# Last stage: GpSimd's whole copy of the odd stack replaced by transfers from two queues

## What is computed

```python
x = x + _L0_conv_ref(_gn(x), ...)     # masked convolution along rows, then a recurrence over the 32 rows
x = x + _L1_conv_ref(_gn(x), L1_conv_W, L1_conv_b, 4)

is3x3 = (i - n) % p == 0              # p = 4: output channel n and input channel i of one class
Wm = W * where(is3x3, full 3x3, centre tap only)
y = conv(x, Wm, padding 1) + sum(b, axis=1)
```

## Time and profile before

| | us |
|---|---|
| three runs | 640.96, 640.69, 638.35 |
| median | 640.69 |
| the profiled execution | 638.67 |
| its span, first to last instruction | 636.9 |
| around the span | 1.8 |
| GpSimd busy in the span | 405.2 |
| TensorE busy in the span | 581.3 |

### The profile page before, as it was taken

One profiled execution on the slowest core, in us unless ns is written; L12 is line 12 of the kernel. 1 busy time (PEld: TensorE's weight loads), 2 busy tenths in 40 slices (PEclk: granted clock), 3 DMA queues, 4 the chain that ended last, 5 costly groups with the idle time before them and its releaser, 6 DMA issues.

```text
span 636.9 us, 19612 instructions
## 1 busy us (share of the span) xinstructions
PE 581.3 (91%) x7741; PEld 381.7 (60%) x7741; DVE 504.3 (79%) x1183; ACT 488.9 (77%) x871; POOL 405.2 (64%) x373
## 2 busy tenths in 40 slices
PE   1799979799999999999999999996799999999995
PEld 0344435378888888878888888884443444343432
DVE  4689884379999999999999999998886686766440
ACT  2579859799999999999999999997374654636440
POOL 1379848545555555554555555554479999999991
PEclk9799979999999999999999999997899999999998
DMA  9988940004124444134442244400057465664755
GB/s 222 263 231 265 238 67 1 4 3 67 35 34 67 67 67 63 31 42 67 67 68 39 30 67 66 68 2 1 21 121 178 114 161 148 142 167 116 172 127 151
DMA packets 89659, 61.47 MB, mean 97 GB/s; under 512 B 73952, under 2 KB 75232, under 8 KB 89568
## 3 DMA queue, kind: packets, MB, share of 16 engines
q1 hardware_dynamic: 88608, 58.90, 44.2%
q10 hardware_dynamic: 960, 1.31, 0.8%
HBM read 35.07 MB, written 16.78 MB: 81 GB/s over the span
## 4 chain that ended last, share of the span: by engine, by line
PE 58%; POOL 23%; DVE 8%; ACT 5%; issue 3%; SPq 1%; DMA 1%; POOLq 0%; DVEq 0%; ACTq 0%
PE ps L1190 18%; PE ps L1168 13%; POOL stack L878 11%; PE ps L1195 9%; PE ps L1172 6%; POOL stack L874 6%; POOL stack L873 5%; PE ps L1113 4%; PE ps L1114 4%; DVE bn L465 2%; SPq L307 1%; PE ps L1290 1%; DMA img<-in_x_dram 1%; PE ps L1248 1%; POOL lo L817 1%
## 5 line engine op out<-in xcount | busy, mean ns | idle before, releaser
L836 POOL TENSOR_TENSOR fc<-gate,cell 128x352 f32<-128x352 f32 (+16 forms) x96 | 83.8, 873 | 142.7 <-ACT gate L978 142.7
L1190 PE MATMUL ps<-z_hi,wg_hi 128*128 128x352 f32 (+13 forms) x384 | 134.0, 350 | 3.1 <-ACT z_hi L962 3.1
L1190 PE MATMUL ps<-z_hi,wg_lo 128*128 128x352 f32 (+13 forms) x384 | 122.1, 319 | 0.0
L1195 PE MATMUL ps<-z_lo,wg_hi 128*128 128x352 f32 (+13 forms) x384 | 107.4, 320 | 0.0
L978 ACT ACTIVATE gate<-ps,gate_bias 128x352 f32<-128x352 f32 (+16 forms) x192 | 104.1, 542 | 1.1 <-PE ps L1195 0.9
L978 ACT ACTIVATE ps<-ps,gate_bias 128x352 f32<-128x352 f32 (+16 forms) x192 | 99.5, 518 | 0.0
L846 POOL TENSOR_TENSOR img<-hT,xr 128x352 f32<-128x352 f32 (+1 forms) x96 | 88.6, 923 | 5.7 <-DVE hT L682 5.6
L1034 ACT ACTIVATE img<-ps,finish 128x512 f32<-128x512 f32 x32 | 23.1, 773 | 88.5 <-PE ps L1290 80.4
L817 POOL TENSOR_TENSOR lo<-xn,hi 128x1024 f16<-128x1024 f32 x32 | 68.0, 2133 | 32.3 <-ACT hi L914 31.7
L465 DVE BATCH_NORM_STATS2 bn<-img 128x6 f32<-128x512 f32 x120 | 75.8, 681 | 5.1 <-DMA img<-in_x_dram 5.0
L1190 PEld LDWEIGHTS ps<-z_hi,wg_hi 128*128 128x128 f32 x384 | 72.3, 188 | 10.1 <-issue 2.6
(11 more groups left out here) (141 smaller groups left out, 1309.7 us busy)
## 6 DMA issues: line engine op xcount, KB each, us to landing
xr<-in_x_dram SPq DMA_DIRECT2D x64, 256.0 KB, 5.4
img<-in_x_dram SPq DMA_DIRECT2D x126, 128.0 KB, 3.4
out_dram<-img SPq DMA_DIRECT2D x62, 256.0 KB, 4.2
stack<-pad SPq DMA_DIRECT2D x46, 134.2 KB, 2.9
stack<-pad_first SPq DMA_DIRECT2D x14, 134.2 KB, 2.8
raw_c<-in_L_conv_W_dram SPq DMA_DIRECT2D x4, 144.0 KB, 3.0
out_dram<-img ACTq DMA_DIRECT2D x2, 256.0 KB, 4.6
img<-in_x_dram ACTq DMA_DIRECT2D x2, 128.0 KB, 3.5
```

What stands on the lines that cost most here:

```text
L836: pool.tensor_tensor(fc[it % 2][:, 0:c1 - c0], gate[it % 2][0][:, 0:c1 - c0], cell[:, c0:c1], ALU.mult).then_inc(fc_done, 1)
L1190: pe.matmul(gbank(it, m)[:, 0:n], w[:, GATE_ORDER[m], :], z_hi[it % 2][:, 0:n], start=(w is wg_hi), stop=False)
L1195: pe.matmul(gbank(it, m)[:, 0:n], wg_hi[:, GATE_ORDER[m], :], z_lo[it % 2][:, 0:n], start=False, stop=True).then_inc(gate_ready, 1)
```

## The change

Three things, all in the last stage, images 2 to 31:

- GpSimd no longer copies `pad` into the odd stack; per image it makes one whole copy and two quarter copies, all into the even stack.
- SyncE's two lowered quarters wait for `lo_done` of the image, and from image 6 on for `conv_done` of the buffer's last user, instead of for GpSimd's copy.
- ScalarE issues two new transfers per image (`stack_odds`): natural quarters 1 and 3 from `pad` into the odd stack, 32 partitions of 2,214 float16 each, with the same waits. They stand behind `norm` of the second image of each pair; for images 2 and 3 ahead of the first group's finish. TensorE waits for them with one more semaphore per buffer, `odd_in`.

The number of transfers for the stacks goes from 60 to 120; GpSimd's instructions go down by 30.

```diff
--- before.py
+++ after.py
@@ -260,7 +260,7 @@
         conv_done = sem("conv_done")
         class_set = sem("class_set")
         blocks_in = sem("blocks_in")
-        odd_stacked = sem("odd_stacked")
+        odd_in = [sem(f"odd_in{i}") for i in range(SLOTS)]
         even_stacked = sem("even_stacked")
         even_below = sem("even_below")
         below_in = [sem(f"below_in{i}") for i in range(SLOTS)]
@@ -409,7 +409,9 @@
 
             def stack_below(b):
 
-                sp.wait_ge(odd_stacked, b - PAIR + 1)
+                sp.wait_ge(lo_done, b + 1)
+                if b >= PAIR + SLOTS:
+                    sp.wait_ge(conv_done, (b - SLOTS) // PAIR + 1)
                 for q in ODD:
                     sp.dma_start(below(b, q), rows_below(b, q)).then_inc(below_in[b % SLOTS], 16)
 
@@ -869,10 +871,7 @@
                     pool.wait_ge(conv_done, (b - SLOTS) // PAIR + 1)
                 if b > PAIR:
                     pool.wait_ge(even_below, len(EVEN) * (b - PAIR))
-                evens, odds = stack[b % SLOTS]
-                pool.tensor_copy(odds[:].bitcast(F32), pad[b % SLOTS][:].bitcast(F32)).then_inc(odd_stacked, 1)
-                pool.tensor_copy(evens[:].bitcast(F32), pad[b % SLOTS][:].bitcast(F32)).then_inc(even_stacked, 1)
-                pool.wait_ge(odd_stacked, b - PAIR + 1)
+                pool.tensor_copy(stack[b % SLOTS][0][:].bitcast(F32), pad[b % SLOTS][:].bitcast(F32)).then_inc(even_stacked, 1)
                 pool.wait_ge(even_stacked, b - PAIR + 1)
                 for q in EVEN:
                     pool.tensor_copy(below(b, q).bitcast(F32), rows_below(b, q).bitcast(F32)).then_inc(even_below, 1)
@@ -1028,6 +1027,16 @@
                     act.wait_ge(lo_done, b - PAIR + 1)
                 whiten(rows(xn[b % PAIR][:]), b, chunk_of(b)[0] % 2, chunk_of(b)[1]).then_inc(xn_done, 1)
 
+            def stack_odds(b):
+
+                act.wait_ge(lo_done, b + 1)
+                if b >= PAIR + SLOTS:
+
+                    act.wait_ge(conv_done, (b - SLOTS) // PAIR + 1)
+                for q in ODD:
+                    r = slice(32 * q, 32 * q + 32)
+                    act.dma_start(stack[b % SLOTS][1][r], pad[b % SLOTS][r]).then_inc(odd_in[b % SLOTS], 16)
+
             def finish_class(g, q):
 
                 act.wait_ge(conv_done, g + 1)
@@ -1048,6 +1057,8 @@
             norm(2)
             high(3)
             norm(3)
+            stack_odds(2)
+            stack_odds(3)
             act.wait_ge(finish_done, 1)
             for g in range(GROUPS):
                 k = (g + 3) // 2
@@ -1067,6 +1078,8 @@
                 if near < B:
                     high(near + 1)
                     norm(near + 1)
+                    stack_odds(near)
+                    stack_odds(near + 1)
             act.wait_ge(out_act, len(ACT_CLASSES) * GROUPS)
             act.wait_ge(out_dve, len(DVE_CLASSES) * GROUPS)
             store_group(act, GROUPS - 1, range(2, Q))
@@ -1277,6 +1290,7 @@
 
                 for b in range(PAIR * g, PAIR * g + PAIR):
                     pe.wait_ge(below_in[b % SLOTS], 16 * len(ODD) * ((b - PAIR) // SLOTS + 1))
+                    pe.wait_ge(odd_in[b % SLOTS], 16 * len(ODD) * ((b - PAIR) // SLOTS + 1))
                 pe.wait_ge(even_below, len(EVEN) * (PAIR * g))
                 for m, (w, part) in enumerate(TERMS):
                     for e in range(3):
```

## The result

The changed kernel took 645.46 us (median of four runs, 641.14 to 649.22), beside 639.61 for the kernel before: a ratio of 1.010, 95% interval 1.0065 to 1.0135, so slower by 1%. Its profiled execution was the fastest of the four, 641.14 us with a span of 639.0, and shows less of the loss than the others had. The same kernel was therefore run and profiled once more among the experiments, with 643 to 647 expected of it: 644.76 us, ratio 1.0103 (1.007 to 1.0137), its profiled execution 644.98 with a span of 642.9. The first profile is called A1 here, the second A2. Before, the span was 636.9.

A forecast was written before the change was run, and what follows sets the result against it. GpSimd's copies were taken as the bound, TensorE only just behind: 6.3 us of waits go, less 0.7 (ScalarE) and 2.8 (program packets), 3.0 us with rounding up, from 640.69 to 637.7 us; range 633.5 to 645.

The forecast's parts named there:

- GpSimd: Last stage: losing the odd copy saves 2.2 us a group, to 9.0; TensorE's 6.3 us of waits go.
- SyncE's quarters, landing: Lowered quarters wait for `lo`, leave earlier or as now, land 2.9 us after issue; cost nothing, hidden by 3.3 us.
- Rival E: Odd stack lands too late, so a transfer wait replaces GpSimd's; no gain, 640.7 us; chance 0.04.
- ScalarE: Natural quarters behind the second `norm`, 1.17 us a pair: nothing to 0.5 us a group; 0.7 us charged once, first iteration.
- C: ScalarE becomes the loop, issue 1.73 us a pair, group 10.9 to 11.1 us; 639 to 642 us; chance 0.10.
- The DMA engines: Last stage: four more transfers a group add 2.4 us of engine time; busy share rises from 0.61 to 0.86.
- TensorE's program: Last stage: instruction packets come late beside fuller DMA engines; stalls three times today's 1.4 us, 2.8 more; bounds 0 to 9.5.
- rival D: TensorE starves at packet ends in stacked and following dense matmuls; 644.6 us at 0.78 a group, 648 at 1.0; chance 0.22.
- over 8 means D: Sign: TensorE's idle ended by "issue" is 4 to 5 us if the forecast holds; over 8 means starvation.
- TensorE's group without waits is not 10.4 us: Condition for being wrong: last-stage group of 11.22 us less 0.80 of waiting gives TensorE's own need, 10.42 us.
- B: The waits simply go, packets no later than now, nothing added to the 1.4 us: gain 5.6, 635.1 us; chance 0.20.

The follow-up runs named there:

- one-queue kernel: Changed kernel with all natural quarters issued by SyncE behind the lowered ones, none by ScalarE: 639.03 us, ratio 1.0017; second set 640.48, 1.0024.
- half of the added bytes: Changed kernel with natural quarters by transfer for each pair's first image only, from SyncE; GpSimd copies the second's odd stack: 638.54 us, ratio 0.9987.
- before with spare transfers: Kernel before plus ScalarE's four transfers a group with the changed kernel's waits, into an unread device-memory array; GpSimd still copies: 644.0 us, ratio 1.0087.
- two store queues beside one stack queue: Changed kernel with all stack transfers from SyncE and two of each group's four stores from ScalarE: 638.36 us, ratio 1.0001.

## Why the prediction was wrong, step by step

The forecast was 637.7, the time 645.46, just over the end of the range. Its mechanism and its list of terms held; one term was mis-sized, and a part of the excess, which depends on who issues the transfers, has no shown cause.

*GpSimd.* Right. All 6.3 us of waits went, also in the version with ScalarE's copy, which gained 4.5 us with that alone.

*SyncE's quarters, landing.* Cost nothing on the path, as said, though 2.9 us to landing became 4.3. Rival E is out: no matmul waits for a transfer.

*ScalarE.* No loop (C is out: its class finish waited 78.4 us for TensorE in A1, 5.6 a group where the forecast said one or two). The one late finish in the first iteration was foreseen at 0.7 and cost 1.4 us, since the pair took 1.90 us to issue, not 1.17; SyncE issued its own pair at the same time. (Of the 2.0 us of A2, 0.54 is a second wait, at a packet end, so it may be the program's.) A2, ScalarE's queue, its class finish, and the dense matmuls:

```profile
470.42 1.90 ACTq L1038 DMA_DIRECT2D stack<-pad  x2
472.37 1.45 ACT L1043 ACTIVATE img<-ps,finish 128x512 f32<-128x512 f32 x2 [4.35 <-issue]
```

```profile
473.19 0.40 PE L1261 MATMUL ps<-pad_first,wall_hi 128*32 128x512 f16 x2 [1.45 <-ACT img L1043]
```

*The DMA engines.* Foreseen 0.86; A1 had 0.73 and A2 0.75:

```profile
500.00:630.00 130.00, 121.94 (x3616) 49.48 (x3608) 72.20 (x140) 63.87 (x68) 81.55 (x66) 1.00 0.75 191
```

So the load rose less than the forecast said, and the harm was greater.

*TensorE's program: the step that failed.* The term was 2.8 us, three times today's stalls, with the busy share taken as a proportion and the value put near the lower of the bounds 0 to 9.5. It measured 7.0 to 7.3 (A1), inside the bounds, and 10.3 to 12.0 (A2), over the upper one. With today's 1.4 that is (10.3 + 1.4) / 14 = 0.84 us a group in A2, 0.96 by the larger balance, between the two prices of rival D (0.78 and 1.0, 644.6 and 648 us): D is what happened. Its reason, a second queue beside SyncE's, isn't shown, for the one-queue kernel has issue rows as long.

A proportion was the wrong form, because a packet that comes in time costs nothing, however near to late it is. Worked out from the q8 packets and the starts of TensorE's rows behind 480 us (a packet's first row is taken from the stalls, with some 255 rows to a packet between them): a packet lasts TensorE 3.3 to 5.9 us, the transfer of the next ends on average 2.25 us after the first row of the current one before the change and 2.91 after it (A2), and TensorE goes on about 1.4 us after a transfer has ended. The mean moved by 0.7 us, but the packets that needed over 3.2 us went from 2 of 33 to 9 of 32. One trace of each kernel:

| kernel (profiled execution, us) | mean us to the end of the next packet's transfer | over 3.2 us |
|---|---|---|
| before, half the stores (637.13) | 1.81 | 0 of 32 |
| changed, half the stores (635.74) | 2.23 | 1 of 33 |
| before (638.67) | 2.25 | 2 of 33 |
| odd stack of first image by ScalarE (634.04) | 2.43 | 1 of 32 |
| half of the added bytes (636.65) | 2.45 | 4 of 32 |
| natural quarters from SyncE (637.86) | 2.73 | 5 of 32 |
| changed, A1 (641.14) | 2.82 | 7 of 33 |
| before with spare transfers (641.89) | 2.87 | 8 of 32 |
| changed, A2 (644.98) | 2.91 | 9 of 32 |
| natural quarters from SyncE, second set (642.46) | 2.96 | 9 of 32 |

The order is nearly that of the bytes that the kernels move, and it doesn't follow who issues them. The argument for the low value was that 13 of 15 groups showed no stall; it would have been better to ask how near to stalling they were.

Against the prediction's own marks: "over 8 means D", and A2's issue row is 9.1; A1's, 5.2, stands just over the 4 to 5 of the forecast, so a single profile could have misled. "Wrong if TensorE's group without waits is not 10.4 us": that number was one group's. From the class finish of group 1 to the last one the kernel before takes 629.24 - 472.00 = 157.24 us for 14 groups, less 6.3 + 1.4 of waits 10.7 each; no term of the sum hangs on it. And the time of the kernel before came out at 639.61 beside the 640.69 of its first three runs, which moves the forecast by 1 us.

*The rules beside B and D.* The Trainium skill, "Runtime: NRT & Kernel Launch", section "Instruction fetch mechanics", calls the crossing of a 16 KiB boundary mostly hidden. Most packets of the kernel before agree; the stalls of 0.47 to 1.57 us above, at packet ends, do not, and half the stores show that it depends on what else the DMA engines carry. The rule of the Trainium skill, "DMA: Bandwidth & Descriptors", section "Issuing engines are not separate DMA queues", that a second queue saves only issue time, agrees with the two store queues beside one stack queue (638.36), and not with the 5 us between ScalarE's and SyncE's natural quarters, of which issue time on ScalarE explains 1 to 2.

## What to carry to other kernels

An engine that runs straight-line code is fed by the same DMA engines as the data, so before transfers are put in place of an idle-looking engine's copies, look at the idle time that ends by "issue" and at the busy share around it. Here such a cost had a threshold: measure how early the program's packets come, not only how many were late. Copies that move to an engine with free time in the stage take no such room; here ScalarE's copy gained 4.5 us where the transfers lost 6. And a profile that differs from the median by some us, as A1 did, is taken again before terms are read from it.

## What the runs showed of the hardware

- With 128 rows put into the program, the stalls moved by 126 rows of the work and stayed where they were in the program; between stalls lie multiples of some 255 rows.
- Stalls of TensorE at packet ends ended 1.3 to 1.7 us after the transfer of a packet (18 in A1 and A2, 2 in the kernel before).
- A pair of stack transfers that ScalarE and SyncE began at the same instant took 1.90 us on ScalarE and 1.91 on SyncE (A2, 470.42); SyncE's pairs alone took 1.14 to 1.73 in the kernel before. That the one slows the other isn't shown: pairs from SyncE's queue alone took up to 3.0 in the one-queue kernel.
- ScalarE copied 128x2214 float16 in 2.04 us, beside GpSimd's 1.11 for the same bytes as 128x1107 float32.
- Two kernels with the same bytes, the same DMA work and other issuers differ by some 5 us (639.03 and 640.48 against 645.46 and 644.76), with issue rows alike (7.0 and 9.8 against 5.2 and 9.1); 1 to 2 us of that is ScalarE's time, 3 to 4 us have no shown cause.
